# Five full tiles of the first twelve batches mapped and worked before the last routing

## Chip, cores and metric

The kernel runs on one core of one Trainium2 chip. The metric is the device time of one execution in microseconds (us); lower is better. A profile is one execution with a record of every instruction. TensorE does matrix products, VectorE and ScalarE elementwise work and reductions, GpSimd elementwise work and indirect DMAs, and SyncE issues DMAs.

## What is computed

The reference is two layers of a gated cross-attention model. There are 16 batches of 128 tokens with 128 features, and 77 context rows for each batch. Each layer adds a gated attention and a gated feed-forward block to `x`; the feed-forward block of the second layer is a mixture of eight experts, of which each token uses one:

```python
x = x + tanh(g_xattn[0]) * _L0_xattn_ref(ctx_1024, _layernorm(x), mask, ...)
x = x + tanh(g_ffn[0])   * _L0_ffn_ref(_layernorm(x), ...)
x = x + tanh(g_xattn[1]) * _L1_xattn_ref(_layernorm(x), ctx_1024, ...)   # top 32 of 77 scores
x = x + tanh(g_ffn[1])   * _L1_ffn_ref(_layernorm(x), Wr, br, W1, W2)
# _L1_ffn_ref, x as [2048, 128]:
route = jax.nn.sigmoid(x @ Wr + br)              # [2048, 8]
max_prob, max_ind = route.max(axis=1), route.argmax(axis=1)
for e in range(8):
    out += (max_ind == e) * (gelu(x @ W1[e]) @ W2[e])   # 128 -> 512 -> 128
out = out * max_prob
```

All is float32.

## The kernel before

Batches run through a software pipeline. `run_steps` calls `step(i, at)` for i = 0 to 20; in step i six stages work on six batches: P on batch i, A on i-1, A2 on i-2, B on i-3, C on i-4 and E on i-5. Each step has eight slots, and each engine has its own `step` with its share of the slots written out by hand, so the order on an engine is the order of the program, and semaphores tie the engines together. Steps 16 to 20 drain the pipeline: in step 19 C works on batch 15 and E on batch 14, and step 20 has only E, for batch 15. Stage E ends with the router: a layer norm (`rsqrt` on GpSimd, `normal` on VectorE), a turn of the rows (`router_T`), the logits (`logits`), and their copy to SBUF (`keep_logits`, semaphore `lg_ready`).

The mixture is sorted. Batches are routed in three groups, `ROUTES = ((0, 11), (11, 15), (15, NB))`. For each group VectorE adds the bias (`route_biases`, L1610), ScalarE takes an exponential (`route_exps`), VectorE picks the expert (`choose`, L1620 to L1628), TensorE counts with small bfloat16 matmuls how many earlier tokens took the same expert (`count_rows`, L1013 and L1017), and VectorE turns that into a row number (`row_places`, L1641 to L1644). GpSimd then writes each batch's 128 rows into the HBM tensor `z_sorted` with one indirect DMA (`place_row`, L617). Every expert has its own region there, 16 tiles long. The first group is routed in step 17 and its rows are written one batch to a slot from step 18 on (`PLACE_AT`); the second group is routed in step 20; the third, batch 15, behind the last step. Only then does `count_rows` add the totals of all experts (L1021), and `map_tiles` works out for each of `SORTED` = 23 tiles which expert it belongs to (`tile_expert`) and where it starts (`tile_row`). A tile is 128 sorted rows; the last tile of each expert is partly empty, and its empty rows carry a token number that the output DMA drops.

Then the tile loop runs. SyncE reads `tile_row` and loads a tile (`load_tile`, L383 and L386; a ring of `RING` = 12). ScalarE reads `tile_expert` and loads that expert's first weights (`load_up`, L1408, 256 KB; a ring of `UPS` = 3). TensorE turns the tile (`turn_z`, L718), multiplies it with the first weights (`tile_up`, L1163) and the result with the second (`tile_down`, L1173); ScalarE applies gelu in between; VectorE copies the turned tile (`z_out`, L1768) and makes the output (`output_out`, L1773); GpSimd scatters it to the output (L706). TensorE's order in the loop is up of tile n+1, turn of tile n+2, down of tile n.

SyncE's loads wait for the whole map and for all 16 scatters:

```python
sp.wait_ge(s["map_ready"], 2)
sp.wait_ge(s["rows_placed"], 16 * NB)
for n in range(SORTED):
    load_tile(n)
```

## Time and profile before

| | us |
|---|---|
| median of 3 runs | 728.25 (727.86 to 730.04) |
| the profiled execution | 727.75 |
| its span | 726.0 |
| TensorE busy in the span | 648.3 (89%) |
| VectorE busy | 571.3 (79%) |
| ScalarE busy | 482.0 (66%) |
| GpSimd busy | 448.7 (62%) |

The span runs from the first to the last recorded instruction; the rest of the execution's time, 1.75 us, lies around it. Busy shares are means over stages with different limits, so the tail is read by itself below. The granted clock is the share of TensorE's full clock that it was given: 1.00 is 2.4 GHz and 0.50 is 1.2 GHz.

### The profile page before, as it was taken

The page shows a single profiled execution, that of the slowest core. Times are in us where ns is not written, and L with a number is a line of the kernel's source. Part 1 is how long each engine was busy: PE and PEld are TensorE (multiplying, and loading weights), DVE is VectorE, ACT ScalarE, POOL GpSimd, SP SyncE. Part 2 cuts the span into 40 slices and gives each one's busy share as a digit, 9 for nine tenths or more (in the row PEclk, how much of TensorE's full clock was granted, in tenths as well). Part 3 has the DMA queues.
Part 4 walks back from the last instruction along what each step waited for, and adds up shares of the span by engine and source line. Part 5 has one row for each costly group of instructions (what it writes and reads, how often), then busy time and mean ns, then how long its engine had stood idle before and what let it go on. Part 6 is the DMA issues. An engine that isn't in the chain of part 4 may idle for free.

```text
span 726.0 us, 19295 instructions
## 1 busy us (share of the span) xinstructions
PE 648.3 (89%) x4994; PEld 528.0 (73%) x4994; DVE 571.3 (79%) x3740; ACT 482.0 (66%) x1331; POOL 448.7 (62%) x689
## 2 busy tenths in 40 slices
PE   6778999999999999999999999999999776771995
PEld 4646577778878786878787878778786755551995
DVE  3276639899999999898989899999999898943231
ACT  2266578787978788887878887978788533221231
POOL 8465677865767575757676575767675546543354
PEclk9799999999999999999999999999999855555898
DMA  7300079990000000000000000000000000003772
GB/s 208 75 1 1 1 201 296 325 282 4 2 2 1 1 1 0 0 0 0 0 0 0 0 0 0 0 0 0 0 1 2 1 0 30 30 23 102 213 225 61
DMA packets 38537, 37.92 MB, mean 52 GB/s; under 512 B 3633, under 2 KB 34249, under 8 KB 38484
## 3 DMA queue, kind: packets, MB, share of 16 engines
q1 hardware_dynamic: 32986, 27.76, 13.7%
q10 hardware_dynamic: 3994, 6.36, 3.0%
q0 software_dynamic: 1504, 3.17, 1.2%
q8 instruction: 24, 0.39, 0.2%
q14 instruction: 29, 0.24, 0.1%
HBM read 16.28 MB, written 21.45 MB: 52 GB/s over the span
## 4 chain that ended last, share of the span: by engine, by line
PE 48%; DVE 35%; issue 6%; POOL 3%; SPq 3%; DMA 2%; ACT 2%; DVEq 0%; another core or an unknown queue 0%; POOLq 0%
DVE sw L1566 14%; DVE m L1560 10%; PE bank L718 8%; PE bank L876 6%; PE bank L947 5%; PE bank L818 5%; PE bank L886 4%; DVE negmax L1513 3%; PE bank L1163 3%; PE score_banks L848 3%; PE bank L1173 3%; PE bank L828 2%; PE bank L806 2%; PE bank L910 2%; PE bank L901 2%
## 5 line engine op out<-in xcount | busy, mean ns | idle before, releaser
L1566 DVE MATCH_REPLACE8 sw<-m,sw 128x77 f32<-128x77 f32 x1024 | 219.8, 222 | 0.1
L1560 DVE MAX8 m<-sw 128x8 f32<-128x77 f32 x1024 | 188.9, 225 | 2.3 <-ACT sw L1191 1.3
L1191 ACT ACTIVATE prob<-score_banks,negmax 128x205 f32<-128x205 f32 x256 | 107.5, 433 | 22.1 <-DVE negmax L1513 22.1
L485 POOL TENSOR_TENSOR prob<-prob,inv 128x820 f32<-128x820 f32 x64 | 99.5, 1554 | 18.6 <-DVE inv L1518 18.6
L504 POOL TENSOR_TENSOR sw<-sw,m 128x616 f32<-128x616 f32 x64 | 78.0, 1218 | 50.0 <-DVEq L1547 49.7
L947 PEld LDWEIGHTS bank<-v,p1T 77*128 77x128 f32 x512 | 72.5, 216 | 15.6 <-DVE c_z L1592 5.2
L947 PE MATMUL bank<-v,p1T 77*128 (+1 forms) x512 | 72.3, 269 | 10.2 <-DVE c_z L1592 4.4
L1566 DVE MATCH_VALUE_LOAD sw<-m,sw 128x8 f32 x1024 | 76.9, 75 | 0.0
L1513 DVE TENSOR_REDUCE negmax<-score_banks 128x2 f32<-128x410 f32 x128 | 68.1, 573 | 2.7 <-PE score_banks L848 2.7
L718 PE MATMUL bank<-ident,prob 128*77 128x128 f32 (+1 forms) x512 | 67.3, 274 | 1.6 <-POOL prob L485 1.4
L828 PE MATMUL bank<-raw,kvT 128*77 128x512 f32 (+1 forms) x128 | 66.7, 603 | 0.0
L1191 ACT ACTIVATE h_ring<-bank 128x256 f32<-128x256 f32 (+1 forms) x87 | 38.5, 443 | 42.3 <-PE bank L1163 31.4
L718 PEld LDWEIGHTS bank<-ident,prob 128*77 128x77 f32 (+1 forms) x512 | 58.7, 146 | 9.3 <-POOL prob L485 5.2
L818 PE MATMUL bank<-kvT,raw 128*128 128x205 f32 x256 | 61.0, 362 | 1.2 <-DVE xs L1525 0.6
L930 PE MATMUL bank<-second_keys,b_q 128*128 128x308 f32 x128 | 53.2, 500 | 9.1 <-ACT p1T L1191 8.2
L848 PE MATMUL score_banks<-k_sb,q_sb 64*128 64x205 f32 x512 | 58.6, 348 | 0.0
L511 POOL TENSOR_TENSOR p<-sw 128x308 f32<-128x308 f32 x64 | 47.0, 735 | 18.0 <-ACT sw L1191 17.8
L876 PE MATMUL bank<-ptc,z_ring 77*64 77x128 f32 x512 | 53.1, 284 | 3.3 <-issue 2.6
L818 PEld LDWEIGHTS bank<-kvT,raw 128*128 128x128 f32 x256 | 43.7, 194 | 16.3 <-issue 14.5
L1191 ACT ACT_TABLE_LOAD x34 | 43.6, 1283 | 17.6 <-issue 17.0
L1191 ACT ACTIVATION_READ_ACCUMULATOR prob<-score_banks,negmax 128x1 f32 x256 | 53.0, 207 | 0.0
L1191 ACT ACTIVATE p1T<-bank 77x512 f32<-77x512 f32 x64 | 37.8, 591 | 19.7 <-PE bank L718 16.3
(235 smaller groups left out, 1457.4 us busy)
## 6 DMA issues: line engine op xcount, KB each, us to landing
z_sorted<-no_row SPq DMA_DIRECT2D x1, 17415.0 KB, 65.5
raw<-in_L_ffn_W ACTq DMA_DIRECT2D x23, 256.0 KB
z_ring<-z_sorted SPq DMA_DIRECT2D x23, 129.0 KB, 2.8
w<-in_L_ffn_W SPq DMA_DIRECT2D x8, 256.0 KB, 4.6
raw<-in_L_xattn_Wkv SPq DMA_DIRECT2D x2, 512.0 KB, 9.1
xs<-in_x SPq DMA_DIRECT2D x1, 960.0 KB, 6.9
cx<-in_ctx SPq DMA_DIRECT2D x1, 577.5 KB
raw<-in_L_xattn_Wq SPq DMA_DIRECT2D x1, 512.0 KB, 8.2
```

Source lines behind the costliest of these rows:

```text
L485: g.tensor_tensor(p, p, inv[:, 4 * q:4 * q + 4].unsqueeze(2).to_broadcast([128, 4, KV]), ALU.mult).then_inc(s["p_norm"], 1)
L504: g.tensor_tensor(v, v, m8[:, 4 * q:4 * q + 4, 0, 0:1].to_broadcast([128, 4, 2 * NK]), ALU.subtract).then_inc(s["sub_done"], 1)
L718: return nc.tensor.transpose(dst, src, ident[0:rows, 0:rows])
L818: last = mm(dst[:, KV * c:KV * c + KV], wkv_in[:, at:at + 128], kvT[:, :], start=True, stop=True)
L828: mm(dst[0:nr, :], kvT[:, r0:r0 + nr], wkv_in[:, INNER + 512 * j:INNER + 512 * j + 512], start=True, stop=True)\
L848: last = mm(SC[:, u, KV * r:KV * r + KV], q_sb[rows[u], q // 2, 2 * (q % 2) + r, :], k_sb[rows[u], q % 2, r, :], start=False, stop=(r == 1 ...
L876: last = mm(dst[64 * u:64 * u + 64, 128 * c:128 * c + 128], v[:, DH * h:DH * h + DH], p[:, 2 * c + u, :], start=not last_part, stop=last_p ...
L947: last = mm(M[:, c:c + D1 + 1], p1T[:, n, :], v1[:, bass.ds(b, 1), 4 * q + n, :].squeeze(1), start=True, stop=True)
L1191: return nc.scalar.activation(dst, src, f, **kw)
L1513: v.tensor_reduce(negmax[:, 2 * p:2 * p + 2], SC[:, :, KV * (p % 2):KV * (p % 2) + KV], AX_X, ALU.max, negate=True).then_inc(s["max_ready" ...
L1560: v.max(m8[:, h, r, :], sw[:, h, src, :]).then_inc(s[name], 1)
L1566: v.match_replace(sw[:, h, 1, :], m8[:, h, r, :], sw[:, h, src, :], TAKEN)\
```

## The change

The first group of batches becomes twelve batches long. Of 12 x 128 = 1536 rows shared among eight experts, at least `FULL` = 5 tiles are full whatever the routing. A new map, `map_full`, lists five such tiles from the first group's totals alone; VectorE works it out at the start of step 20. SyncE loads these tiles once twelve scatters have landed, ScalarE loads their weights in step 20 (the ring `UPS` grows to 5), TensorE turns tile 0 in step 20 (slot 4) and tile 1 behind step 20, and runs tile 0's up matmuls ahead of the third count. `map_rest` lists the other 18 tiles. It leaves out the tiles already taken, and everything behind tile 4 waits for it (`map_ready` 4) and for the other four scatters (the new semaphore `rows_late`). The total counting matmuls now run for the first group also. The load semaphores `ld_wk`, `ld_wv`, `ld_wout` are merged into `ld_wq`, and `ld_router` into `ld_ffnb`, to free four.

```diff
-    UPS = 3
+    UPS = 5
-    ROUTES = ((0, 11), (11, 15), (15, NB))
+    ROUTES = ((0, 12), (12, 15), (15, NB))
+    FULL = -(-(ROUTES[0][1] * S - NE * (S - 1)) // S)
...
             sp.wait_ge(s["map_ready"], 2)
-            sp.wait_ge(s["rows_placed"], 16 * NB)
-            for n in range(SORTED):
+            sp.wait_ge(s["rows_placed"], 16 * ROUTES[0][1])
+            for n in range(FULL):
+                load_tile(n)
+            sp.wait_ge(s["map_ready"], 4)
+            sp.wait_ge(s["rows_late"], 16 * (NB - ROUTES[0][1]))
+            for n in range(FULL, SORTED):
                 load_tile(n)
...
-                                     rows_out[:, b, :], None).then_inc(s["rows_placed"], 16)
+                                     rows_out[:, b, :], None)\
+                    .then_inc(s["rows_placed" if n == 0 else "rows_late"], 16)
...
-                if b1 == NB:
-                    for b in range(NB):
-                        last = mm(S1[:, 0:NE], ones_bf[:, :], chosen[:, b, :], start=(b == 0), stop=(b == NB - 1))
+                if n != 1:
+                    for b in range(b1):
+                        last = mm(S1[:, 0:NE], ones_bf[:, :], chosen[:, b, :], start=(b == 0), stop=(b == b1 - 1))
...
                     if i == 20 and slot == 4:
                         count_rows(1)
+                        pe.wait_ge(s["map_ready"], 2)
+                        turn_z(0)
...
-            count_rows(2)
-
-            pe.wait_ge(s["ld_w2"], 16 * NE)
-            pe.wait_ge(s["map_ready"], 2)
-            turn_z(0)
+            reach(pe, "lg_ready", NB - 1, 1)
             turn_z(1)
             tile_up(0)
+            count_rows(2)
+            pe.wait_ge(s["ld_w2"], 16 * NE)
             for n in range(SORTED):
                 if n + 1 < SORTED:
                     tile_up(n + 1)
                 if n + 2 < SORTED:
                     turn_z(n + 2)
+                if n == FULL:
+                    pe.wait_ge(s["map_ready"], 4)
                 tile_down(n)
...
                     if i == 20 and slot == 0:
                         route_exps(1)
+                        act.wait_ge(s["map_ready"], 2)
+                        for n in range(2):
+                            load_up(n)
...
                     if slot == 3:
                         if E is not None:
                             move(E, c_zT, "cT_psum", "cT_ready")
+                        if i == 20:
+                            for n in range(2, FULL):
+                                load_up(n)
...
-                if n + UPS < SORTED:
-                    load_up(n + UPS)
+                if n == FULL - 3:
+                    act.wait_ge(s["map_ready"], 4)
+                    load_up(FULL)
+                    load_up(FULL + 1)
+                if n > FULL - 3 and n + UPS - 1 < SORTED:
+                    load_up(n + UPS - 1)
...
+                    if (i, slot) == (20, 0):
+                        map_full()
                     if (i, slot) in ((17, 0), (20, 0)):
                         route_biases(0 if i == 17 else 1)
...
                     if (i, slot) in ((17, 7), (20, 5)):
                         row_places(0 if i == 17 else 1)
+                    if (i, slot) == (20, 5):
+                        z_out(0)
...
             route_biases(2)
             choose(2)
+            z_out(1)
             row_places(2)
-            map_tiles()
-            z_out(0)
-            z_out(1)
-            for n in range(SORTED):
-                if n + 2 < SORTED:
-                    z_out(n + 2)
+            z_out(2)
+            map_rest()
+
+            z_out(3)
+            output_out(0)
+            for n in range(1, SORTED):
+                if n + 3 < SORTED:
+                    z_out(n + 3)
                 output_out(n)
```

`map_full` is 17 operations of VectorE. 13 of them set `map_ready` to 2, and the other four prepare what `map_rest` needs. `map_rest` has 12 operations of the old map's kind on 18 tiles:

```diff
+            def map_full():
+                spread = [128, FULL, NE]
+                past, skip = t_past[:, 0:FULL, :], t_skip[:, 0:FULL, :]
+                then(v.tensor_scalar(t_exp[:, 0:NE], S1[:, 0:NE], 1.0 - S, None, ALU.add))
+                then(v.tensor_tensor(n_full[:, :, :], t_exp[:, 0:NE].unsqueeze(2).to_broadcast([128, NE, NB]),
+                                     steps_128[:, :].unsqueeze(1).to_broadcast([128, NE, NB]), ALU.is_gt))
+                then(v.tensor_reduce(f_tiles[:, :], n_full[:, :, :], AX_X, ALU.add))
...
+                v.tensor_tensor(tile_row[:, 0:FULL], t_row[:, 0:FULL], tile_no[:, 0:FULL], ALU.add)\
+                    .then_inc(s["map_ready"], 1)
+                v.tensor_scalar(tile_expert[:, 0:FULL], t_exp[:, 0:FULL], NE - 1.0, None, ALU.min)\
+                    .then_inc(s["map_ready"], 1)
+                then(v.tensor_scalar(f_end[:, NE:NE + 1], f_end[:, NE - 1:NE], 0.0, None, ALU.add))
+                v.tensor_tensor(f_next[:, :], f_end[:, 1:NE + 1], f_end[:, 0:NE], ALU.subtract)
...
+            def map_rest():
...
+                v.tensor_tensor(skipped[:, :], f_next[:, :], n_tiles[:, :], ALU.subtract)
...
+                then(v.tensor_tensor(end[:, :], end[:, :], f_end[:, 0:NE], ALU.subtract))
...
```

## Rows read from the trace of the kernel before

**Rows 1.** The page: span; granted clock in 40 slices (tenths of full speed).

```profile
span 726.0 us, 19295 instructions
...
PEclk9799999999999999999999999999999855555898
```

**Rows 2.** Tail stages: busy PE, PEld, DVE, ACT, POOL; clock, DMA share, GB/s.

```profile
666.60:671.13 4.53, 0.45 (x1) 0.18 (x2) 0.29 (x1) 1.28 (x1) 0.00 (x0) 0.50 0.76 231
671.13:682.82 11.69, 11.63 (x77) 11.38 (x78) 2.51 (x8) 2.99 (x5) 2.95 (x3) 0.76 0.70 211
682.82:718.64 35.82, 35.61 (x315) 35.09 (x313) 11.63 (x36) 10.75 (x18) 17.71 (x19) 1.00 0.66 188
```

**Rows 3.** The chain that ended last, 656 to 676: start, us, what.

```profile
656.82 0.19 ACT route L1191
...
659.08 2.71 another core or an unknown queue
...
662.84 2.59 DMA z_sorted<-rows_out,place
...
667.59 3.49 DMA z_ring<-z_sorted
...
671.61 3.42 PE bank L1163 x16
```

**Rows 4.** VectorE in order of time, 596 to 666: start, us, instruction, [idle before].

```profile
596.92 0.38 DVE L1560 MAX8 m<-sw 128x8 f32<-128x77 f32 x2 [0.29 <-DVE sw L1566]
...
599.16 1.84 DVE L1644 CAST place<-place_f 128x11 uint32<-128x11 f32 x1
...
642.37 0.34 DVE L1538 TENSOR_SCALAR r_z<-rows_out,c_mv,c_rs 128x128 f32<-128x128 f32 x1 [1.16 <-POOL c_rs L493]
646.74 0.19 DVE L1610 TENSOR_TENSOR route<-route,br 128x32 f32<-128x32 f32 x1 [4.03 <-ACT route L1191]
...
654.82 0.35 DVE L1538 TENSOR_SCALAR r_z<-rows_out,c_mv,c_rs 128x128 f32<-128x128 f32 x1 [0.41 <-POOL c_rs L493]
...
662.48 0.28 DVE L1650 TENSOR_TENSOR n_full<-score_banks,steps 128x128 f32<-128x128 f32 x1
...
665.20 0.17 DVE L1664 TENSOR_SCALAR tile_expert<-t_exp 128x23 int32<-128x23 f32 x1
```

**Rows 5.** GpSimd in order of time: the last scatter of step 19, the root.

```profile
638.91 0.99 POOL L617 DMA_INDIRECT z_sorted<-rows_out,place  x1 [0.17 <-issue]
...
641.41 0.19 POOL L491 TENSOR_SCALAR c_rs<-c_mv 128x1 f32<-128x1 f32 x1 [0.18 <-DVE c_mv L1534]
```

**Rows 6.** TensorE in order of time, 591 to 683.

```profile
591.61 1.40 PE L930 MATMUL bank<-second_keys,b_q 128*128 128x308 f32 x2 [0.22 <-ACT p1T L1191]
...
643.14 0.42 PE L718 MATMUL bank<-ident,r_z 128*128 128x128 f32 x1
644.19 1.88 PE L947 MATMUL bank<-v,p1T 77*128 77x9 f32 x8 [0.63 <-ACT r_zT L1191]
...
655.31 0.45 PE L718 MATMUL bank<-ident,r_z 128*128 128x128 f32 x1 [2.32 <-DVE r_z L1538]
...
682.82 1.06 PE L1163 MATMUL bank<-z_T,raw 128*128 128x128 f32 x8
```

**Rows 7.** ScalarE in order of time; ACTq is its queue, issuing weight loads.

```profile
651.33 0.28 ACT L1191 ACTIVATE c_zT<-bank 128x128 f32<-128x128 f32 x1 [3.12 <-PE bank L718]
655.80 0.28 ACT L1191 ACTIVATE r_zT<-bank 128x128 f32<-128x128 f32 x1 [4.19 <-PE bank L718]
...
666.60 2.50 ACTq L1408 DMA_DIRECT2D raw<-in_L_ffn_W  x3
...
678.50 0.34 ACTq L1408 DMA_DIRECT2D raw<-in_L_ffn_W  x1
```

**Rows 8.** Issue to landing: tile loads (L386), the second weights' loads (L373).

```profile
DMA to landing us min/median/max: 2.4/2.8/4.0
...
DMA to landing us min/median/max: 2.6/4.6/5.8
```

More of the change, by code:

```diff
@@ L47, in flamingo_kernel @@
     NOWHERE = 1 << 20
-    ROUTES = ((0, 11), (11, 15), (15, NB))
+    ROUTES = ((0, 12), (12, 15), (15, NB))
+    FULL = -(-(ROUTES[0][1] * S - NE * (S - 1)) // S)
+    assert FULL == UPS and (NB * S - FULL * S + NE * (S - 1)) // S <= SORTED - FULL
     assert S == 128 and D == 128 and DH == 64 and HID == 512 and NK * 4 <= 512
@@ L191, in flamingo_kernel @@
         end = sb("end", [128, NE])
+        f_tiles = sb("f_tiles", [128, NE])
+        f_end = sb("f_end", [128, NE + 1])
+        f_next = sb("f_next", [128, NE])
+        tile_from = sb("tile_from", [128, SORTED - FULL])
         skipped = sb("skipped", [128, NE])
@@ L367, in _ @@
             sp.dma_start(dn_bias[:, :], row("L0_ffn_down_bias")).then_inc(s["ld_ffnb"], 16)
-            sp.dma_start(wr[:, :], t["L1_ffn_Wr"]).then_inc(s["ld_router"], 16)
-            sp.dma_start(br[:, :], row("L1_ffn_br")).then_inc(s["ld_router"], 16)
+            sp.dma_start(wr[:, :], t["L1_ffn_Wr"]).then_inc(s["ld_ffnb"], 16)
+            sp.dma_start(br[:, :], row("L1_ffn_br")).then_inc(s["ld_ffnb"], 16)
             sp.wait_ge(s["dn_done"], NST)
@@ L779, in _ @@
                 wait_job(pe, k)
-            for name in ("ld_wq", "ld_wk", "ld_wv", "ld_wout"):
-                pe.wait_ge(s[name], 16)
+            pe.wait_ge(s["ld_wq"], 64)
             reader, now = {}, dict(step=0, at=None)
@@ L1018, in count_rows, with turn_z, tile_up, tile_down @@
                               stop=(k == b1 - 1), skip_group_check=True)
-                if b1 == NB:
-                    for b in range(NB):
-                        last = mm(S1[:, 0:NE], ones_bf[:, :], chosen[:, b, :], start=(b == 0), stop=(b == NB - 1))
+                if n != 1:
+                    for b in range(b1):
+                        last = mm(S1[:, 0:NE], ones_bf[:, :], chosen[:, b, :], start=(b == 0), stop=(b == b1 - 1))
                 last.then_inc(s["count_psum"], 1)
+            def turn_z(n):
+                pe.wait_ge(z_loaded[n % RING], 16 * (n // RING + 1))
+                if n >= 2:
+                    pe.wait_ge(s["zT_ready"], n - 1)
+                turn([X, M][n % 2][:, 0:128], z_tile[:, n % RING, 0:D]).then_inc(s["zT_psum"], 1)
+            def tile_up(n):
+                pe.wait_ge(s["zT_ready"], n + 1)
+                pe.wait_ge(up_loaded[n % UPS], 16 * (n // UPS + 1))
+                if n >= 2:
+                    pe.wait_ge(s["hT_ready"], n - 1)
+                dst = [GZ, TC][n % 2]
+                for c in range(HC):
+                    last = mm(dst[:, 128 * c:128 * c + 128], w1_tile[:, n % UPS, 128 * c:128 * c + 128], z_T[:, n % 2, :],
+                              start=True, stop=True)
+                last.then_inc(s["up_psum"], 1)
+            def tile_down(n):
+                e = pe.value_load(tile_expert[0:1, n:n + 1], min_val=0, max_val=NE - 1)
+                pe.wait_ge(s["hT_ready"], n + 1)
+                if n >= 2:
+                    pe.wait_ge(s["ey_ready"], n - 1)
+                for c in range(HC):
+                    last = mm([TL, OA][n % 2][:, 0:D], hT[:, n % 2, c, :], w2[:, bass.ds(e, 1), c, :].squeeze(1),
+                              start=(c == 0), stop=(c == HC - 1))
+                last.then_inc(s["ey_psum"], 1)
             def step(i, at):
@@ L1143, in _ @@
             run_steps(pe, step, LAGS + 1)
+            reach(pe, "lg_ready", NB - 1, 1)
+            turn_z(1)
+            tile_up(0)
             count_rows(2)
             pe.wait_ge(s["ld_w2"], 16 * NE)
[L1148 to L1179 removed]
             for n in range(SORTED):
@@ L1404, in _ @@
             route_exps(2)
-            def load_up(n):
-                e = act.value_load(tile_expert[0:1, n:n + 1], min_val=0, max_val=NE - 1)
-                act.dma_start(w1_tile[:, n % UPS, :], t["L1_ffn_W1"][bass.ds(e, 1)].squeeze(0))\
-                    .then_inc(up_loaded[n % UPS], 16)
-            act.wait_ge(s["map_ready"], 2)
-            for n in range(UPS):
-                load_up(n)
             for n in range(SORTED):
@@ L1644, in row_places @@
                 v.tensor_copy(place[:, b0:b1], place_f[:, b0:b1]).then_inc(s["place_ready"], 1)
-            def map_tiles():
+            def map_full():
[5 more added lines that the diff above has]
+                then(v.tensor_reduce(f_tiles[:, :], n_full[:, :, :], AX_X, ALU.add))
+                v.tensor_scalar(skipped[:, :], f_tiles[:, :], float(NB), -1.0, ALU.subtract, ALU.mult)
+                then(v.tensor_tensor(n_before[:, :, :], before_e[:, :, :],
+                                     f_tiles[:, :].unsqueeze(1).to_broadcast([128, NE, NE]), ALU.mult))
+                then(v.tensor_reduce(end[:, :], n_before[:, :, :], AX_X, ALU.add))
+                v.tensor_scalar(f_end[:, 0:NE], end[:, :], float(FULL), None, ALU.min)
+                then(v.tensor_tensor(past, tile_no[:, 0:FULL].unsqueeze(2).to_broadcast(spread),
+                                     end[:, :].unsqueeze(1).to_broadcast(spread), ALU.is_ge))
+                then(v.tensor_tensor(skip, past, skipped[:, :].unsqueeze(1).to_broadcast(spread), ALU.mult))
+                v.tensor_reduce(t_exp[:, 0:FULL], past, AX_X, ALU.add)
+                then(v.tensor_reduce(t_row[:, 0:FULL], skip, AX_X, ALU.add))
+                v.tensor_tensor(tile_row[:, 0:FULL], t_row[:, 0:FULL], tile_no[:, 0:FULL], ALU.add)\
[4 more added lines that the diff above has]
+                v.tensor_tensor(f_next[:, :], f_end[:, 1:NE + 1], f_end[:, 0:NE], ALU.subtract)
+                then(v.tensor_tensor(tile_from[:, :], tile_no[:, 0:SORTED - FULL],
+                                     f_end[:, 0:1].to_broadcast([128, SORTED - FULL]), ALU.add))
+                then(v.tensor_scalar(f_next[:, :], f_next[:, :], float(NB), None, ALU.add))
```

89 lines of the change are left out of this document (35 added, 54 removed).

## The prediction

> **What bounds the kernel now.** I read the page first, then the busy time by stage of the tail, then the chain that ended last, and then each engine's order of time around the place where the change acts. The profiled span is 726.0 us, and TensorE's granted clock has sunk to half in it from 581 us on [rows 1]. The last part of the span has three stages. Up to about 657 us the sixteenth batch (number 15) goes through its last attention step and its router, on a chain in which every engine takes turns. From 657 to 671.13 us TensorE is almost empty: the chain goes from the copy of the last logits (ends 657.01) over the choice of experts, a count on TensorE (2.71 us), the last scatter of rows (2.59), SyncE's read of the map, and the load of the second sorted tile (3.49) to the first tile's matmuls [rows 2, 3]. From 671.13 us on TensorE is full: 35.61 of the 35.82 us up to 718.64. That is tile work: 313 weight loads, 17 to a tile, in 35.82 us make 1.95 us a tile. Its beginning ran at half clock: the mean grant of 671.13 to 682.82 is 0.76, so the clock was 1.2 GHz for 11.69 x 0.24 / 0.5 = 5.6 us and then 2.4 [rows 2]. The sixth tile's up matmuls begin at 682.82 [rows 6]. What the change is worth is how much earlier than 682.82 they begin, since everything behind them is the same work at the same pace.
>
> **The change part by part.**
>
> *Step 17.* Twelve batches are routed instead of eleven. TensorE's first count gets one matmul more and twelve for the totals. The count of 32 such pairs took 2.71 us [rows 3], 85 ns each, so 13 add 1.1 us. Behind it stands a score matmul that began at 591.61; its result is first used by VectorE at 596.92, so some 3 us of cover hide it [rows 4, 6]. If that cover were gone it would cost 1.1. VectorE's ten or so wide operations grow by one batch of 8 columns in 88: 0.1 us on the chain. Merging the load semaphores costs nothing: these loads are long done.
>
> *Step 19.* One scatter more stands on GpSimd between the subtraction for batch 15 and the variance root of batch 14. A scatter holds GpSimd 0.99 us and the next instruction starts 1.11 after its start at the earliest [rows 5]. The root starts at 641.41, so it and the normalised rows (642.37) come 1.1 us later. TensorE turned those rows at 643.14, 0.3 us after it could have, then waited for ScalarE and began the next contexts at 644.19 [rows 4, 6]. With the rows at 643.8, the turn at 644.0 and its copy, I get 644.85: 0.7 us later, and TensorE's order carries that to batch 15's end. Bounds: 0 (if the slack is larger than the rows show) and 1.1.
>
> *Step 20, VectorE.* The map of the full tiles is 17 small operations. The old map's 11 took 662.48 to 665.37, 0.26 each with waits [rows 4]; 13 of the new ones come before the tiles are known (2.6 us on narrower tiles than those), 4 behind. They start after the normalised rows of batch 14, now 643.8, so the map is known at 646.5 and done at 647.3. VectorE stood idle from 642.7 to 646.74 there, and the next operation now waits for logits at 647.4 [rows 4]: cost 0. Without that cover it would be 3.4. The copy of tile 0 (0.3) goes in ahead of the normalising at 654.82, where 0.41 is idle [rows 4]: 0, or 0.3 if it misses.
>
> *Step 20, ScalarE.* Two expert loads go ahead of its copy at 651.33, before which it was idle for 3.12, and three ahead of the copy at 655.80, after 4.19 idle. Three loads took 2.5 us of its queue and began 1.2 after the map [rows 7], so two need 2.9 at most and three 3.7: 0; if one slips, up to 1.
>
> *Step 20, SyncE and TensorE.* Between the landing of the last rows (662.84 + 2.59 = 665.43) and the turn of the first tile TensorE waited 3.9 us: SyncE's reads and a load, whose landing takes 2.4 to 4.0 [rows 3, 8]. With the map at 646.5 tile 0 is there at 650.4. TensorE asks for it after its second count, where it stood idle 2.32 us before 655.31 for the normalised rows of batch 15 [rows 6]: from 653.0, now about 653.9, so there are 3.5 us of slack and the turn falls into idle time. Cost 0. Queued behind that wait are the router's turn and logits of batch 15, and everything after them.
>
> *The hole.* The logits are copied at 657.01 + 0.8 = 657.8. TensorE turns tile 1 (0.45) and runs tile 0's up (1.71, half of the 3.42 that two took cold [rows 3]) until 660.0; the third count, which could have started at 659.9, follows and takes 2.7: 662.7. Tile 1's up ends at 664.0 to 664.4. VectorE works out the last row places until 663.5, and the scatter of batch 15 lands at 663.8 + 2.6 = 666.4. VectorE must take tile 2's turn (664.5 to 665.0) before it starts the last map. That is 12 operations, 2.8 us: known at 667.3 to 667.8, where before it was 665.37. The map is then what tile 5 waits for, the scatter is not.
>
> *Tile 5.* Its rows are on hand 3.9 us after the map: 671.2 to 671.7. Its weights are issued after ScalarE's third activation, 1.2 us behind the map, at 668.5 to 669.6; in the tail a load issued after an activation was used 4.3 us later without a stall (issued 678.50 and used 682.82), and the eight similar loads of the second weights landed in 2.6 to 5.8 [rows 7, 8]. That gives 672.8 to 673.9. TensorE's own order (five ups and four downs with their turns) reaches tile 5 at 672.2 if the clock rises 5.6 us after 657.8, and at 672.8 if it rises 5.6 us after the count. I take 673.2 for tile 5's up.
>
> **The sum.** 682.82 - 673.2 = 9.6 us earlier, the 0.8 of steps 17 and 19 already inside. The span becomes 716.4. The profiled execution took 727.75 with 1.75 outside its span, and the median is 728.25, 0.5 above it; the forecast is 728.25 - 9.6 = **718.6 us**. Favourable ends (no delay in step 19, weights in 2.6): tile 5 at 671.4, 716.8. Unfavourable ends (weights in 5.8 behind the late map, 0.9 more from the slips): 676.3, 721.7.
>
> **Rivals.**
>
> *The clock stays at 1.2 GHz through the five tiles (13 in 100).* For it: in five slices of 18 us, from 581 to 671, it was at half although TensorE worked in all of them [rows 1], and the new work has waits in it. Against it: the work from 657.8 has no hole, and uninterrupted work raised it before. A cold tile takes 2 x 1.71 + 0.2 = 3.6; four of these after 662.7 put tile 5's up at 677.1, a gain of 5.7: 722.5.
>
> *TensorE stands at tile 5 (10 in 100).* The rows or the weights come 2 to 3 us after my figure because 18 tile loads start while the weights load, as when the load of tile 1 took 3.49 with the DMA share at 0.76 [rows 2, 3]. Gain 6.6 to 7.6: about 721.2.
>
> *Batch 15 is held in step 20, and the kernel is slower (4 in 100).* The wait for tile 0 stands in TensorE's order before the router of batch 15. It costs nothing while tile 0 lands before 654, then one for one. It cancels the gain of 9.6 when tile 0 lands 13 us late, at 664; with 5 us more it gives 733. It needs the twelfth scatter, issued near 641.5, to land about 15 us late. The trace has something of this kind: a VectorE cast of 11 columns beside GpSimd's key spreading took 1.84 us instead of 0.15 [rows 4]. The Trainium skill, SBUF — State Buffer, section "Who interferes with whom", has the mechanism: the two engines share one port pair, held for a whole instruction, and GpSimd needs it to write a scatter's descriptors. By that rule VectorE's new scalar operations and GpSimd's copies at 643 to 645 delay each other; the row above agrees. If each of them lost 1.7, the map would come 2 us later and still leave slack, so I give this little.
>
> *The tiles are worked early and nothing moves (2 in 100).* That is so if the tail is bound by its transfers and not by TensorE. Against it: TensorE is 99% busy there at a DMA share of 0.66 [rows 2]. It would give 728 to 729.
>
> **How the numbers follow.** The forecast has 71 in 100 with 716.8 to 721.7. With the first two rivals (up to 722.5) I reach 94, so a range of **716.6 to 722.6** leaves out the last two, and some for what I have not seen. About 0.3%, 2 us, is what a measurement of this kernel can tell from no change. Faster by more: 0.94. Within: 0.02. Slower: 0.04.
>
> **What would show it.** The profile of the changed kernel should show tile 0's turn near 654, the logits' copy about 0.8 later than 657.0, tile 0's up before the third count, the second map ending at 667 to 668, tile 5's up near 673 and the granted clock at 2.4 GHz from 663 to 669. If the gap before tile 5 exceeds 1 us, the data path was mis-sized; if tiles 2 to 4 take 3.6 us each, the clock was; if the last logits are later than 659, step 19 or 20 holds batch 15. The forecast falls if any of those is off by more than 3 us.

## The result, and the profile of the changed kernel

The changed kernel took 717.19 us, the median of four runs (716.98 to 718.71), against 728.06 us (727.37 to 730.04, four runs) for the kernel before on the same chip. The ratio of the runs is put at 0.9835, with a 95% interval of 0.9813 to 0.9858; the two medians by themselves give 0.985. Two repeats on other chips gave 0.984 [0.9812, 0.9867] and 0.9831 [0.9807, 0.9855]. The forecast was 718.6 us (a ratio of 0.9868) with a range of 716.6 to 722.6: the direction was right and the size too small. The median itself lies inside the range, but 0.9835 of the 728.25 us that the forecast started from is 716.2, 0.4 below its low end. The profiled execution took 717.09 us, with a span of 715.3 against 726.0, so 10.7 us less. The forecast had said 9.6. So the gain is 10.7 us by the profile, 10.9 by the medians and 12.0 by the ratio.

The page of the changed kernel, beside [rows 1]:

```profile
span 715.3 us, 19341 instructions
...
PEclk9989999999999999999999999999999965555998
```

The busy time by stage of the tail (columns as in [rows 2]), cut at the last logits' copy, at the rise of the clock, and at tile 5's up:

```profile
657.98:663.90 5.92, 5.86 (x55) 5.74 (x56) 3.03 (x17) 2.69 (x5) 3.07 (x4) 0.50 0.20 70
663.90:672.51 8.61, 6.85 (x56) 6.29 (x56) 3.79 (x17) 1.79 (x3) 2.17 (x3) 1.00 0.50 159
672.51:706.50 33.99, 33.99 (x307) 33.96 (x305) 9.69 (x35) 10.77 (x18) 17.50 (x18) 1.00 0.68 204
```

In the kernel before, TensorE was empty from its count to 671 us but for one turn at 669.33. Now it is 99% busy in the first of these stages, 80% in the second (6.85 of 8.61 us) and all the time in the third. The granted clock rose to 2.4 GHz at 663.9, 5.9 us after that work began, and stayed there. The order of time of TensorE shows the filled hole (start, us, instruction, idle before it in brackets; L730 is a turn, L1048 an up, L1058 a down, L1024 to L1032 the last count):

```profile
657.20 0.57 PE L985 MATMUL bank<-wr,r_zT 128*128 128x8 f32 x2 [0.46 <-ACT r_zT L1203]
658.04 0.48 PE L730 MATMUL bank<-ident,z_ring 128*128 128x128 f32 x1 [0.27 <-ACT route L1203]
658.31 1.92 PE L1048 MATMUL bank<-z_T,raw 128*128 128x128 f32 x8
660.08 0.17 PE L1024 MATMUL score_banks<-chosen,before_p 128*128 128x8 bf16 x1
660.10 0.55 PE L1028 MATMUL score_banks<-chosen,ones_bf 128*128 128x8 bf16 x15
660.51 0.57 PE L1032 MATMUL score_banks<-chosen,ones_bf 128*128 128x8 bf16 x16
660.93 2.06 PE L1048 MATMUL bank<-z_T,raw 128*128 128x128 f32 x8
...
668.62 1.06 PE L1048 MATMUL bank<-z_T,raw 128*128 128x128 f32 x8
670.62 0.33 PE L730 MATMUL bank<-ident,z_ring 128*128 128x128 f32 x1 [0.94 <-DMA z_ring<-z_sorted]
671.52 1.15 PE L1058 MATMUL bank<-w,h_ring 128*128 x8 [0.58 <-issue]
672.51 1.06 PE L1048 MATMUL bank<-z_T,raw 128*128 128x128 f32 x8
```

Tile 5's up starts at 672.51, where [rows 6] has 682.82: 10.3 us of the 10.7. The other 0.4 lies in the tile loop behind it. The kernel before has three uneven moments there: its ups follow each other every 1.90 us, but for three that come 2.26 (694.20 and 696.46), 2.02 and 1.97 after the one ahead. The changed kernel has one of 1.96 at tile 6 and none behind 674.47.

### The profile page after: what moved, and what is told of

It is laid out like the page before. It is cut to its first block, busy times and chain, and to the rows that moved or that the text cites. A ratio compares the mean times of both kernels' runs of the same rounds, so it can differ in the third digit from the quotient of the medians.

```text
span 715.3 us, 19341 instructions
## 1 busy us (share of the span) xinstructions
PE 646.1 (90%) x5007; PEld 525.3 (73%) x5007; DVE 572.8 (80%) x3758; ACT 482.1 (67%) x1331; POOL 447.6 (63%) x689
## 3 DMA queue, kind: packets, MB, share of 16 engines
q1 hardware_dynamic: 32986, 27.76, 13.8%
## 4 chain that ended last, share of the span: by engine, by line
PE 48%; DVE 34%; issue 7%; POOL 5%; SPq 3%; ACT 1%; DMA 1%; DVEq 0%; POOLq 0%
DVE sw L1585 13%; DVE m L1579 9%; PE bank L730 8%; PE bank L887 6%; PE bank L829 5%; PE bank L958 5%; PE bank L897 4%; DVE negmax L1532 3%; PE score_banks L859 3%; PE bank L1048 3%; PE bank L839 2%; PE bank L1058 2%; PE bank L817 2%; PE bank L921 2%; PE bank L912 2%
## 5 line engine op out<-in xcount | busy, mean ns | idle before, releaser
L496 POOL TENSOR_TENSOR prob<-prob,inv 128x820 f32<-128x820 f32 x64 | 99.5, 1554 | 18.6 <-DVE inv L1537 18.6
L730 PE MATMUL bank<-ident,prob 128*77 128x128 f32 (+1 forms) x512 | 67.3, 274 | 1.6 <-POOL prob L496 1.4
L839 PE MATMUL bank<-raw,kvT 128*77 128x512 f32 (+1 forms) x128 | 67.2, 607 | 0.0
L730 PEld LDWEIGHTS bank<-ident,prob 128*77 128x77 f32 (+1 forms) x512 | 58.6, 146 | 9.4 <-POOL prob L496 5.2
L829 PE MATMUL bank<-kvT,raw 128*128 128x205 f32 x256 | 59.4, 355 | 1.2 <-DVE xs L1544 0.6
L1203 ACT ACTIVATE p1T<-bank 77x512 f32<-77x512 f32 x64 | 37.8, 591 | 19.8 <-PE bank L730 16.5
L1203 ACT ACTIVATE sw<-sw 128x616 f32<-128x616 f32 x64 | 46.9, 732 | 5.7 <-POOL sw L515 5.4
```

What stands on the lines that cost most here:

```text
L496: g.tensor_tensor(p, p, inv[:, 4 * q:4 * q + 4].unsqueeze(2).to_broadcast([128, 4, KV]), ALU.mult).then_inc(s["p_norm"], 1)
L730: return nc.tensor.transpose(dst, src, ident[0:rows, 0:rows])
L829: last = mm(dst[:, KV * c:KV * c + KV], wkv_in[:, at:at + 128], kvT[:, :], start=True, stop=True)
L839: mm(dst[0:nr, :], kvT[:, r0:r0 + nr], wkv_in[:, INNER + 512 * j:INNER + 512 * j + 512], start=True, stop=True)\
L1203: return nc.scalar.activation(dst, src, f, **kw)
```

## The experiments

They answer two questions. What is the last count's wait made of, the term that the forecast had mis-sized? And where is what is left of the hole? In the traces I read two intervals: from the count's first matmul to VectorE's row places, and from the copy of the last logits to tile 5's up or to the last output scatter. Both are free of the shift that whole runs show against each other. Runs of one kernel differ in where the tail starts by up to 1.1 us (the last logits are copied at 657.80, 657.31 and 658.37 in three traces of the changed kernel). The times of the whole that are given for an experiment are single runs unless a range or a ratio stands beside them. Beside them the kernel before took 732.42 us (the count and TensorE's idleness), 729.82 (the signal), 731.3 (the scatters and the three tiles) and 728.76 (the parts of a scatter), each on a chip of its own, so only the intervals carry the argument.

**Is the count 85 ns a pair?** Sixteen more pairs for the totals, added to the kernel before and to the changed one.

```diff
-                    for b in range(NB):
+                    for b in list(range(NB)) * 2:
```

> The kernel before, with the 16 totals matmuls of the last count done twice (32 + 16 pairs in all). My prediction took the 2.71 us between the count's start and VectorE's row places as 85 ns a pair on TensorE. If that is right, the wait grows by 1.4 us to 4.1 us and the span with it. Rival: the pairs take 28 ns each, as their starts in the trace lie (0.42 us for 15), and a fixed part of some 1.8 us lies behind them; then the wait grows by 0.4 to 0.5 us.

> The changed kernel, with the 16 totals matmuls of the last count done twice. At 85 ns a pair tile 1's up and the row places come 1.4 us later; at 28 ns 0.4 to 0.5 us later. The span grows by no more than that, and by less if tile 5 has slack.

At 85 ns they would add 1.4 us. Before, the places came 2.87 us after the count's first matmul instead of 2.71 (730.5 us in all); in the changed kernel the next up came 1.42 us after it instead of 0.85, 36 ns a pair, and the places 1.60 instead of 1.51 (718.49 us). So the 2.71 us of [rows 3] is not the work of 32 pairs. It is a wait for something else, with 0.85 us of work in it.

**Does TensorE's idleness around the count make the signal late?** Four float32 matmuls behind the count, or six ahead of it, in the kernel before.

```diff
+            for n in range(6):
+                mm(X[:, 0:128], ident[:, :], ident[:, :], start=True, stop=True)
```

> The kernel before, with four float32 matmuls of no use put directly behind the last count on TensorE (1 us or so at half clock, into a bank that nobody reads). If the pairs are slow by themselves, VectorE's wait stays 2.7 us. If the count's signal is late because TensorE's queue runs empty behind it, as it does not in the changed kernel, the wait falls to about 1.5 us and the span by 1.2.

> The kernel before, with six float32 matmuls of no use put directly ahead of the last count (2.7 us at half clock from 656.8, so the count starts near 659.5 instead of 659.1). If the count is slow because TensorE stood idle before it (the changed kernel has tile 0's up there), the time from the count's start to VectorE's row places falls from 2.7 to about 1.5 us and the row places come 0.8 us earlier. If not, it stays 2.7 and they come 0.4 later.

2.70 and 2.55 us, against 2.71 (729.27 and 730.65 us in all). The matmuls behind the count began 0.86 us after its first one (659.32 and 660.18), while the signal took 2.70: TensorE was through with the count long before. Its own work is not it.

**Is it the signal, or VectorE?** Eight small VectorE operations between the choice and the row places, and a copy on ScalarE that waits for the same count; in the changed kernel the ScalarE copy alone.

```diff
+            act.wait_ge(s["count_psum"], 3)
+            copy(seen[:, :], expert_base[:, :])
...
+            for n in range(8):
+                then(v.tensor_scalar(probe[:, :], expert_base[:, :], 1.0, None, ALU.add))
```

> The kernel before, with eight small independent operations of VectorE (0.2 us each, 1.6 in all) between the choice of batch 15's expert and its row places, and a small ScalarE copy that waits for the third count's signal alone. If TensorE's signal is what takes 2.7 us, VectorE runs its eight back to back from 659.1 to 660.7, then waits, ScalarE's copy and the row places both start near 661.8, and nothing costs time. If the signal comes after 1.0 to 1.1 us and VectorE is slow to go on by itself (its instructions are not there yet), ScalarE's copy runs near 660.2 and a hole of about 1.5 us or more stands among or behind the eight operations.

> The changed kernel, with the same small ScalarE copy that waits for the third count's signal, ahead of tile 0's gelu. It shows when the signal arrives where VectorE's row places started 1.51 us behind the count's first matmul. If TensorE's signal sets that time, the copy runs at 1.5 us behind it; if VectorE is late by itself, at 1.0 to 1.1. Tile 0's gelu moves behind the copy (from 660.3 to about 661.7), still ahead of its use at 663.0, so the time stays within 0.3 us.

In the kernel before with the probes, VectorE and then ScalarE in order of time:

```profile
660.21 1.95 DVE L1766 TENSOR_SCALAR probe<-expert_base 128x8 f32<-128x8 f32 x8
663.16 0.17 DVE L1645 TENSOR_TENSOR place_e<-score_banks,expert_base 128x8 f32<-128x8 f32 x1 [1.00 <-remote]
```

```profile
663.09 0.21 ACT L1193 ACTIVATE seen<-expert_base 128x8 f32<-128x8 f32 x1 [4.44 <-remote]
```

VectorE worked until 662.16, and the two engines went on within 0.07 us of each other, 2.78 (ScalarE) and 2.85 us after the count's first matmul at 660.31 (730.09 us). In the changed kernel both went on at 663.59, 1.48 us after it (719.2 us). It is the signal that is late, in both kernels, and by different amounts.

**Do the row scatters hold it?** Before, four scatters stand on GpSimd at that time; the changed kernel has three, since batch 11 went into the first group. In both, the places start 0.8 to 0.9 us after the last of these ends. GpSimd in the kernel before, and in the changed one (with the scatter of batch 15 last):

```profile
660.02 0.96 POOL L617 DMA_INDIRECT z_sorted<-rows_out,place  x1 [0.31 <-issue]
662.84 0.96 POOL L617 DMA_INDIRECT z_sorted<-rows_out,place  x1 [1.85 <-DVE place L1644]
```

```profile
659.74 0.96 POOL L628 DMA_INDIRECT z_sorted<-rows_out,place  x1 [0.30 <-issue]
662.62 0.96 POOL L628 DMA_INDIRECT z_sorted<-rows_out,place  x1 [1.92 <-DVE place L1663]
```

So I moved them behind the scatter of batch 15, all of them (before and after) or only that of batch 14 (before).

```diff
-        PLACE_AT[20, 6] = tuple(range(*ROUTES[1]))
...
             place_row(NB - 1)
+            for b in range(*ROUTES[1]):
+                place_row(b)
```

> The kernel before, with the row scatters of batches 11 to 14 issued by GpSimd behind that of batch 15 instead of ahead of it, so that no scatter runs while TensorE's last count is done. Before, VectorE's row places start 2.7 us after the count's first matmul, in the changed kernel 1.5 us after it; the one has four scatters ahead of them, the other three, and in both the places start 0.8 to 1.0 us after the last of these ends. Theory of the scatters: the count's signal is held back by them; without them the row places start 1.0 to 1.4 us after the count's first matmul, 1.3 to 1.7 us sooner than before. Rival, the signal takes as long as it does for a reason of the count's own, and its standing 0.9 us behind the scatters is chance: 2.7 us as before. The whole gets no faster by it in either case: the last row scatter is issued at about 665 instead of 663, and the tile loads wait for it, so about +1 us.

> The kernel before, with only batch 14's row scatter moved behind that of batch 15, so that three run ahead of it, as in the changed kernel. Theory of the scatters: the last of the three ends 1.27 us sooner than the fourth does before, and the row places start with it, 1.4 to 1.6 us after the count's first matmul. Rival, a reason of the count's own (its number of matmuls, the work of TensorE around it): 2.7 us.

> The changed kernel, with the row scatters of batches 12 to 14 behind that of batch 15. Theory of the scatters: row places 1.0 to 1.4 us after the count's first matmul instead of 1.5. Rival: 1.5 us. The last map is known by as much sooner, but the last scatter issued about 1.9 us later, and the late tiles' loads wait for both: tile 5's turn at the same time or up to 1.5 us later.

The row places with none ahead and with three ahead, in the kernel before (the counts' first matmuls stand at 659.57 and 661.08):

```profile
660.60 0.17 DVE L1642 TENSOR_TENSOR place_e<-score_banks,expert_base 128x8 f32<-128x8 f32 x1 [1.05 <-PE score_banks L1022]
```

```profile
662.39 0.17 DVE L1642 TENSOR_TENSOR place_e<-score_banks,expert_base 128x8 f32<-128x8 f32 x1 [1.33 <-PE score_banks L1022]
```

| kernel | last scatter ahead ends | count's first matmul | row places | between |
|---|---|---|---|---|
| before, four ahead | 660.98 | 659.10 | 661.81 | 2.71 |
| before, three ahead | 661.70 | 661.08 | 662.39 | 1.31 |
| before, none ahead | | 659.57 | 660.60 | 1.03 |
| changed, three ahead | 660.70 | 660.08 | 661.59 | 1.51 |
| changed, none ahead | | 658.79 | 659.87 | 1.08 |

With nothing ahead the signal takes 1.03 to 1.08 us, 0.85 of it matmuls. With scatters it comes 0.7 to 0.9 us after the end of the last one in this table. (In b_count16 and b_probe it is 0.9 to 1.0.) Where the count itself was long, with its sixteen pairs more in the changed kernel, the signal came 0.18 us behind the work, as with no scatter. The theory stands, and the rival, a cause of the count's own, falls. The scatters' place is right all the same. With them last, the stretch from the last logits' copy to the last output scatter is 67.2 us instead of 63.2 (before) and 56.5 instead of 51.5 (changed), because the late tiles' loads wait for the last row scatter. In the changed kernel with none ahead that one was issued at 664.81, and tile 5's turn came 7.2 us later, at 672.04. The whole took 732.29 us (before) and 720.82 (changed), and 730.97 with three ahead in the kernel before.

**Which part of a scatter holds it?** Again nothing ahead of batch 15's scatter, but five multiplications of 128x516 on GpSimd in one kernel, and four plain transfers of the same rows from SyncE's queue in the other.

```diff
+            reach(sp, "lg_ready", NB - 1, 1)
+            for k in range(4):
+                sp.dma_start(probe_out[128 * k:128 * k + 128, :],
+                             rows_out[:, ROUTES[1][0] + k, :]).then_inc(s["c_token"], 16)
```

> The kernel before without row scatters ahead of batch 15's, but with four plain transfers of the same rows_out tiles to device memory, issued from SyncE's queue when the last logits are there. If the transfers themselves hold the signal of TensorE's count: 1.3 us or more after the count's first matmul. If it is GpSimd's making of the scatters' descriptors: 1.0 to 1.1 us.

> The kernel before without row scatters ahead of batch 15's (as with none ahead, where the row places started 1.03 us after the count's first matmul), but with five multiplications of 128x516 elements on GpSimd at that time, about 1.05 us each. If GpSimd's being busy holds the signal of TensorE's count: 1.5 to 2.7 us. If it is the scatters' transfers or their descriptors: 1.0 to 1.1 us, but for VectorE's own operations being slower beside GpSimd's.

The plain transfers, by stretches of 1 us (columns as in [rows 2]; the count's first matmul is at 659.16, the places at 660.20):

```profile
658.00:659.00 1.00, 0.00 (x0) 0.00 (x0) 0.83 (x7) 0.00 (x0) 0.00 (x0) 0.50 0.80 268
659.00:660.00 1.00, 0.84 (x32) 0.87 (x32) 0.14 (x2) 0.00 (x0) 0.00 (x0) 0.50 0.77 259
```

The DMA engines were 77% busy over the count, and the signal took 1.04 us (732.02 us in all). Plain transfers do not hold it. The run with arithmetic on GpSimd doesn't answer its question. It slowed VectorE's choice so much that the count began at 663.11, 0.17 after GpSimd's work had ended at 662.94; the signal took 1.03 us (737.41 us). So what holds it is something in the scatter that a plain transfer lacks. Whether that is GpSimd's being busy or its making of the scatter's descriptors stays open.

**Is the gain the tiles in the hole?** Three tiles in the early map instead of five, and twenty in the last. The weight ring stays at 5; ScalarE's first late weight loads move one activation later, which the lines below leave out.

```diff
-    FULL = -(-(ROUTES[0][1] * S - NE * (S - 1)) // S)
+    FULL = 3
...
```

> The changed kernel with three full tiles in the early map instead of five, and twenty in the last: the same 23 tiles. Theory that the gain is the hole before the first late tile, filled with tiles at about 1.9 us each: the first late tile (now number 3) is up at the time at which number 5 was, 672.5 with this kernel's start, and two tiles more stand behind it: +3.8 us, 721 us. Rival, that the gain came from the sooner clock or the sooner map, which three tiles bring too: within 1 us of the changed kernel, 717 to 718.

TensorE of that kernel, in order of time:

```profile
664.70 1.06 PE L1048 MATMUL bank<-z_T,raw 128*128 128x128 f32 x8
670.82 0.33 PE L730 MATMUL bank<-ident,z_ring 128*128 128x128 f32 x1 [5.07 <-DMA z_ring<-z_sorted]
671.58 2.07 PE L1058 MATMUL bank<-w,h_ring 128*128 x8 [0.42 <-issue]
673.44 1.55 PE L1048 MATMUL bank<-z_T,raw 128*128 128x128 f32 x8
```

722.19 us (721.52 to 723.64), ratio 0.9882 [0.9859, 0.9905]. From the last logits' copy to the last output scatter it is 56.3 us (658.22 to 714.47) against 51.5 (657.80 to 709.32) and, in the kernel before, 63.2 (656.82 to 720.04). The two tiles that left the hole cost 4.7: 3.8 for themselves, as expected, and about 0.9 more. The clock fell behind the open 5.07 us, so tile 1's down and the beginning of tile 3's up ran at 1.2 GHz. The same kernel by stretches (the granted clock is the third figure from the end):

```profile
668.00:671.00 3.00, 0.18 (x1) 0.14 (x1) 0.00 (x0) 0.60 (x1) 0.00 (x0) 1.00 0.72 214
671.00:674.00 3.00, 2.58 (x12) 2.43 (x12) 0.55 (x2) 0.00 (x0) 1.00 (x1) 0.51 0.96 309
```

So the gain is in the main the tiles in the hole, and five also keep the clock up.

**What is left of it?** Six runs: the changed kernel again beside late_scatter on one chip, and again beside the other three on a second. late_scatter undoes the cost of step 19, map_sooner takes tile 2's copy out from ahead of the last map, down_first works tile 3's second matmuls before tile 5's turn, and all_three does all of it.

```diff
+        PLACE_AT[19, 4] = PLACE_AT.pop((19, 3))
...
-            z_out(2)
-            map_rest()
+            map_rest(lambda: z_out(2))
...
-                if n + 2 < SORTED:
+                if n + 2 < SORTED and n != FULL - 2:
                     turn_z(n + 2)
...
                 tile_down(n)
+                if n == FULL - 2:
+                    turn_z(n + 2)
```

> The changed kernel itself, to have its gain beside the kernel before on this chip: my forecast put the gain at 9.6 us, its profile showed 10.7, and the ratio of its timed runs (0.9835) stands for 12.0. By the profile the ratio should be 0.985 to 0.986.

> The changed kernel, with the scatter of batch 11 moved from the end of slot 3 to the end of slot 4 of step 19, behind the root of batch 14. My step 19 says that the scatter ahead of the root costs 0.7 us; the profile after shows 0.5 (0.97 of delay at the last logits, of which 0.39 was there by 60 us). So the logits' copy should come 0.5 us earlier and the time should fall by 0.5. Rival: the delay comes from elsewhere (the map on VectorE), and nothing moves. Tile 0's rows land 1 us later, where 3 us are to spare.

> The changed kernel, with tile 2's copy of z_T on VectorE moved from ahead of the last map to its middle (behind the sum that gives where each expert's tiles end), so that the map doesn't stand behind the 0.90 us in which VectorE waits for that tile's turn. Theory that the last map binds tile 5: the map is known about 0.8 us sooner and tile 5's turn comes 0.8 us sooner; the whole -0.8 us. Rival, the landing of the last scatter binds (with that scatter moved 1.9 us later, tile 5's turn came 7.2 us after its start; here it starts at 662.62, so not before 669.8 against the 670.62 of the changed kernel): -0.8 us at most, and no more to be had by a still sooner map. Rival, nothing: tile 2's up, delayed, delays the tiles ahead by as much as the map gains, 0.

> The changed kernel, with tile 3's second matmuls issued ahead of tile 5's turn instead of behind it, so that they run in TensorE's wait of 0.94 us for tile 5's rows. Theory that this wait and the 0.58 us behind it are a hole with nothing in it: tile 5's up starts 0.5 to 0.9 us sooner, the whole -0.5 to -0.9 us. Rival, the turn, its copy on VectorE and the up then stand in one chain that nothing covers: 0.

> The changed kernel with batch 11's scatter moved one slot later (the 0.5 us in step 19), tile 2's z_T copy inside the last map, and tile 3's second matmuls ahead of tile 5's turn. If the three costs are what the profile shows and are apart: -0.5 -0.8 -0.6 = -1.9 us against the changed kernel, a ratio to the kernel before about 0.981. Rival: the last two fill the same hole, so -1.3 us. Rival: none of them is on the path that sets the end: 0.

> The changed kernel itself, beside its three variants on one chip: ratio to the kernel before 0.984.

| kernel | us | ratio | batch 14's rows to last logits | to tile 5's up | to tile 7's up | to last scatter |
|---|---|---|---|---|---|---|
| changed, its first profile | 717.19 | 0.9835 [0.9813, 0.9858] | 17.2 | 14.7 | 18.6 | 51.5 |
| changed, after_third | 717.66 | 0.9831 [0.9807, 0.9855] | 17.2 | 14.7 | 18.6 | 51.6 |
| changed, after_again | 718.43 | 0.984 [0.9812, 0.9867] | 17.2 | 14.7 | 19.1 | 52.1 |
| late_scatter | 717.86 | 0.9834 [0.9812, 0.9857] | 16.7 | 14.6 | 18.4 | 51.4 |
| map_sooner | 718.25 | 0.9824 [0.9803, 0.9846] | 17.2 | 13.8 | 18.6 | 51.6 |
| down_first | 717.44 | 0.982 [0.9803, 0.9838] | 17.2 | 13.6 | 19.0 | 52.0 |
| all_three | 716.05 | 0.9807 [0.9786, 0.9828] | 16.7 | 12.4 | 19.8 | 52.8 |

The last four columns are intervals between starts in one trace each, and the last three count from the logits' copy. The kernel before has 16.7 (640.10 to 656.82) in the first of them. late_scatter has that back, so step 19's cost was that scatter; the times of the whole can't show 0.5 us. The other two do what they should at tile 5 (0.9 and 1.1 us sooner, 2.3 with all three), and by tile 7 nothing of it is left. TensorE of the kernel with all three:

```profile
669.94 1.16 PE L1049 MATMUL bank<-z_T,raw 128*128 128x128 f32 x8 [0.38 <-DVE z_T L1725]
671.96 0.33 PE L731 MATMUL bank<-ident,z_ring 128*128 128x128 f32 x1 [0.86 <-issue]
672.80 1.87 PE L1059 MATMUL bank<-w,h_ring 128*128 x8 [0.52 <-issue]
674.47 1.91 PE L1049 MATMUL bank<-z_T,raw 128*128 128x128 f32 x8
```

and its stretches of 2 us:

```profile
670.00:672.00 2.00, 1.14 (x9) 0.95 (x9) 0.14 (x1) 0.60 (x1) 0.98 (x1) 1.00 0.99 346
672.00:674.00 2.00, 1.48 (x7) 1.29 (x8) 0.55 (x2) 0.00 (x0) 0.34 (x1) 0.76 0.97 298
674.00:676.00 2.00, 2.00 (x12) 2.00 (x11) 0.00 (x0) 0.00 (x0) 0.64 (x1) 0.50 0.81 239
```

Tile 5 comes sooner, and tile 6's turn is the next to wait. There was little room already: in one of the three traces of the changed kernel tile 6's up came 2.54 us behind tile 5's instead of 1.96 or 2.08 (673.08 and 675.62 in after_again). The DMA engines are 97 to 99% busy there with the tile and weight loads that all start when the last map is known. That their crowding is what holds tile 6 fits this, but no run takes loads away to show it. With the two waits the clock falls once more. The profile gives none of the variants a gain at the end; all_three's median is 1.6 us below that of the changed kernel beside it, its profiled execution is not, and the intervals overlap. None is shown to be faster.

## Why the forecast was right in kind and too small

*Steps 17 and 19.* As forecast, the longer first count is hidden: VectorE stands 0.4 us late already at 60 us, and 0.48 at 634. The first figure is the shift between executions (the same row starts at 60.53, 61.08 and 60.11 in the three traces of the changed kernel, and at 60.15 in the kernel before). The scatter in step 19 costs 0.5 (forecast 0.7). The last logits are copied at 657.80, against a forecast 657.8 for the copy's end. Counted from the row at 60 us to the last output scatter, and so without the shift, the changed kernel is 11.1 us shorter (659.9 and 648.8; 10.5 and 11.1 in its other two traces). The forecast missed 1.5 of these: 0.9 between the last logits and tile 5's up, 0.2 ahead of the logits, and 0.4 in the tile loop.

*Step 20.* The early map, the copy of tile 0, the five loads and tile 0's turn are hidden, as forecast, the first with little room: the map's tiles are known at 647.0 and its last operation ends at 647.57, 0.23 before the next (VectorE; the second and third row show the map's slow operation and that margin):

```profile
644.13 0.16 DVE L1669 TENSOR_SCALAR t_exp<-score_banks 128x8 f32<-128x8 f32 x1
644.97 0.52 DVE L1673 TENSOR_SCALAR skipped<-f_tiles 128x8 f32<-128x8 f32 x1
647.80 0.18 DVE L1629 TENSOR_TENSOR route<-route,br 128x24 f32<-128x24 f32 x1 [0.23 <-ACT route L1203]
```

The 0.52 us of `skipped` fell beside two GpSimd operations, where its kind takes 0.17 elsewhere. By the Trainium skill, SBUF — State Buffer, section "Who interferes with whom", the two engines share a port pair; this row agrees, and so does the run with GpSimd arithmetic, where VectorE's 0.20 us operation on the chosen experts took 0.71. Batch 15 was not held: tile 0 was turned at 653.75 without a wait.

*The step that failed: the count.* "the third count ... follows and takes 2.7: 662.7" took an interval between two engines for TensorE's work. In [rows 3] the chain names that piece "another core or an unknown queue" and not TensorE, which should have stopped me. The count's work is 0.85 us, 27 ns a pair, so tile 1's up began at 660.93 instead of 662.7. The rest of the 2.71 was a signal held by the scatters ahead. The change itself moved one scatter away and so cut that wait to 1.5 us, a gain of about 1.2 us for the row places that I had not seen. I had divided 2.71 by 32 pairs, and the 1.1 us for step 17's 13 pairs more (hidden, so without effect) has the same error in it. The chain that ended last in the changed kernel (start, us, what) has the count at 0.85 us, and goes from it over tile 2's turn to the last map and not over the row places:

```profile
660.22 0.02 PE score_banks L1024
660.25 0.40 PE score_banks L1028 x15
660.65 0.43 PE score_banks L1032 x16
661.08 1.91 PE bank L1048 x8
662.99 0.23 PE bank L730
663.24 0.29 DVE z_T L1721
```

The Trainium skill, TensorE: Matmul & The Clock Gate, section "Wait — 56ns, not 53.3ns?", gives a floor of about 25 ns from one matmul to the next however few the columns. The 27 ns here lie close to it. A floor doesn't rule out 85, but three times the floor was a reason to look at the starts of the rows.

*What followed from it.* The last map ran 0.9 to 1.4 us sooner. Its VectorE rows:

```profile
661.59 0.17 DVE L1660 TENSOR_TENSOR place_e<-score_banks,expert_base 128x8 f32<-128x8 f32 x1 [1.34 <-PE score_banks L1032]
663.24 0.29 DVE L1721 COPY z_T<-bank 128x128 f32<-128x128 f32 x1 [0.90 <-PE bank L730]
663.45 0.28 DVE L1699 TENSOR_TENSOR n_full<-score_banks,steps 128x128 f32<-128x128 f32 x1
666.21 0.17 DVE L1714 TENSOR_SCALAR tile_expert<-t_exp 128x18 int32<-128x18 f32 x1
```

Known at 666.4 instead of 667.3 to 667.8. The clock rose at 663.9, as forecast for the case without a break. TensorE was through with tile 4's up at 669.7. At 1.9 us a tile from that up's start at 668.62, its own order would have reached tile 5's up at 670.5 instead of the forecast 672.2. It waited 0.94 us for tile 5's rows, whose turn came 4.2 us behind the map (forecast 3.9), and the up began at 672.51.

*The weights.* I had let tile 5's weights decide, at 672.8 to 673.9. They didn't: in down_first that tile's up starts 4.3 us after its load was issued (667.56 and 671.86) and waits only for VectorE's copy. The rows come last. In the changed kernel the load was issued at 667.08, 0.7 us behind the map, where I had 1.2 behind a later map and so 668.5 to 669.6. The favourable end of the range (tile 5 at 671.4) went by fast weights and no delay in step 19, and had the 2.7 us count in it. With the count at 0.85 TensorE's order would have reached tile 5 at 670.4, and the same working would have ended near 717.6, with the low end a microsecond lower.

*A second step that failed: the pace of the loop.* "Everything behind them is the same work at the same pace" put a term at nothing that the longer ring of weight buffers could change. From tile 7's up to the last it takes 28.43 or 28.44 us in all eleven traces with the changed loop, 29.0 in the kernel before, and 29.6 to 31.1 in the eight experiments on it, whose loop is the same. A likely cause is the ring of five weight buffers. With three the load for a tile is issued 3.9 us ahead of its up, with five 5.8 us, and [rows 8] has landings of 2.6 to 5.8. Before, tile 11's load and up, and in the changed kernel tile 16's:

```profile
690.28 0.34 ACTq L1408 DMA_DIRECT2D raw<-in_L_ffn_W  x1
694.20 1.06 PE L1163 MATMUL bank<-z_T,raw 128*128 128x128 f32 x8
```

```profile
687.63 0.34 ACTq L1307 DMA_DIRECT2D raw<-in_L_ffn_W  x1
693.43 1.06 PE L1048 MATMUL bank<-z_T,raw 128*128 128x128 f32 x8
```

No run has the longer ring alone, so this cause is not shown. The profiled execution of the kernel before was the most even of the nine, which may be part of why the ratio of the runs shows more gain than the two profiles do.

*The rivals.* The clock did not stay at 1.2 GHz through the five tiles; with three tiles it fell again, so what that rival describes can happen here. TensorE's wait at tile 5 was 0.94, just under the 1 us that I had set as the sign of a mis-sized data path, and 1.5 with the 0.58 behind it. Behind tile 5 the rival is real: what the variants won ahead of it was gone by tile 7.

## What to carry to other kernels

An interval of the chain that is charged to no engine is a wait, not work. Before dividing it into so many instructions, compare it with the starts of two neighbouring rows on the engine. When work is put into a hole, the gain is the tiles that fit in it until the next map or load; making the hole's end come sooner by itself bought nothing here, with all the loads behind the map starting together. Compare how long before its use each load of a loop is issued with how long such loads take to land: a ring that is lengthened for one reason can pay for another. A queue of scatters beside a short handoff between other engines is worth a look even if none of them waits for it.

## What the runs showed of the hardware

A signal from TensorE to VectorE and ScalarE came 1.03 to 1.08 us after the first matmul of a 0.85 us count where no row scatter ran, 1.3 to 1.5 with three and 2.55 to 2.85 with four, in these cases 0.7 to 1.0 us after the end of the last one. Plain transfers of the same rows, at a DMA share of 0.77, left it at 1.04. Where a turn came late behind a load and a down was next, the down stood about half a microsecond more with no cause in the profile: 0.58, 0.53 and 0.53 in the changed kernel's three traces, 0.51 in map_sooner, 0.52 in all_three, 0.42 with three tiles and 0.37 with no scatter ahead. Why was not tried.
